# A decoder layer on one core: the finished half's stream goes through two PSUM banks, copied by ScalarE and added from there by VectorE

## What is computed

```
x = x + mamba(layernorm(x))                     # selective scan, 16 states, 512 inner channels
x = x + cross_attention(layernorm(x), ctx)      # 154 context tokens
x = ffn(x):                                     # 8 experts, top 2
    xc = x.astype(bfloat16)
    ...
    combined = sum over experts of weight_e * p2_e
    out_ffn = xc + combined.astype(bfloat16)     # a bfloat16 sum
x = x + out_ffn                                  # float32
```

## Time and profile before

| | us |
|---|---|
| median of 3 runs (1624.03 to 1624.16) | 1624.06 |
| the profiled execution, its own time | 1627.51 |
| span of the profiled execution | 1625.7 |
| DVE busy in the span | 1412.4 (87%) |
| PE / POOL / ACT busy | 1246.4 / 972.3 / 950.8 |
| mean granted PE clock | 0.902 |

### The profile page before, as it was taken

How to read it: one execution, slowest core, us unless ns; L and a number is a source line. 1 busy time by engine, 2 the same in 40 slices (tenths; PEclk the granted TensorE clock), 3 DMA queues, 4 the chain that set the end, 5 groups by cost and what they waited for, 6 DMA issues and landing times. The chain is left out here.

```text
span 1625.7 us, 24035 instructions
## 1 busy us (share of the span) xinstructions
PE 1246.4 (77%) x5942; PEld 852.6 (52%) x5942; DVE 1412.4 (87%) x1861; ACT 950.8 (58%) x1401; POOL 972.3 (60%) x529
## 2 busy tenths in 40 slices
PE   4756667779787868898777868788777777886797
PEld 2344444655455545665355545566345555565475
DVE  6589999797799999988699999989689999983697
ACT  2555444244777767524777767814777867722564
POOL 1298888312789878521689878721488978820000
PEclk9879999889798989999799989999889989997699
DMA  7111111401121211311112113221111211220111
GB/s 229 41 46 40 52 58 40 157 1 54 48 75 53 72 59 58 113 42 54 40 46 71 48 53 104 81 76 34 47 59 46 71 46 59 84 101 27 45 60 52
DMA packets 75758, 103.30 MB, mean 64 GB/s; under 512 B 9213, under 2 KB 52614, under 8 KB 75663
## 3 DMA queue, kind: packets, MB, share of 16 engines
q1 hardware_dynamic: 70508, 98.41, 19.1%
q10 hardware_dynamic: 5154, 3.78, 0.7%
HBM read 83.22 MB, written 18.96 MB: 63 GB/s over the span
## 5 line engine op out<-in xcount | busy, mean ns | idle before, releaser
L1804 PE MATMUL ps<-ident,work 128*128 128x128 f32 x1536 | 304.4, 321 | 214.4 <-DVE stage L1404 72.8
L1366 DVE TENSOR_TENSOR_SCAN work<-ps,work 128x1024 f32<-128x1024 f32 x192 | 438.4, 2283 | 27.7 <-ACT ps L966 20.2
L1804 PEld LDWEIGHTS ps<-ident,work 128*128 128x128 f32 x1536 | 191.8, 159 | 350.2 <-DVE stage L1404 124.6
L966 ACT ACTIVATE ps<-dt,a_neg 128x1024 f32<-128x1024 f32 x256 | 285.6, 1118 | 135.6 <-DVE work L1366 85.4
L719 POOL TENSOR_TENSOR work<-dtu,b_bc 128x1024 f32<-128x1024 f32 x128 | 301.8, 2385 | 50.4 <-PE ps L1804 46.5
L1404 DVE SCALAR_TENSOR_TENSOR stage<-ps,c_tok,stage 128x512 f32<-128x512 f32 x384 | 272.2, 733 | 22.2 <-PE ps L1804 20.1
L1826 PE MATMUL ps<-w,work 128*128 (+1 forms) x1024 | 249.5, 389 | 1.8 <-DVE work L1539 1.8
L1826 PEld LDWEIGHTS ps<-w,work 128*128 128x128 f32 x1024 | 195.9, 195 | 38.2 <-DVE work L1539 2.6
L735 POOL TENSOR_TENSOR stage<-stage,work 128x512 f32<-128x512 f32 x128 | 160.7, 1277 | 53.1 <-ACT work L982 53.1
L1776 PE MATMUL ps<-nfT,w 128*128 128x512 bf16 x512 | 165.8, 423 | 33.7 <-DVE work L1472 19.9
L719 POOL TENSOR_TENSOR work<-dtu,w_out 128x1024 f32<-128x1024 f32 x64 | 149.3, 2353 | 47.0 <-PE ps L1804 47.0
(11 more groups left out here) (169 smaller groups left out, 2017.0 us busy)
## 6 DMA issues: line engine op xcount, KB each, us to landing
b_bc<-b_rows SPq DMA_DIRECT2D x32, 512.0 KB, 3.9
w_out<-b_rows SPq DMA_DIRECT2D x32, 512.0 KB, 4.4
wbc<-combine_rows SPq DMA_DIRECT2D x64, 256.0 KB, 3.7
work<-z_rows SPq DMA_DIRECT2D x8, 1024.0 KB, 6.4
z_rows<-mix SPq DMA_DIRECT2D x24, 256.0 KB, 2.7
stage<-in_x SPq DMA_DIRECT2D x8, 512.0 KB, 4.3
xt<-in_x SPq DMA_DIRECT2D x8, 512.0 KB, 3.8
x_rows<-xt SPq DMA_DIRECT2D x4, 1024.0 KB, 4.3
```

The source lines that it names most:

```text
L966: act.activation(decay_in(d, alone, opening), dt[:, d, :], ACT.Exp, scale=a_neg[:, bass.ds(it * 2 + (d * N + hf * (N // 2) + par), 1)]).th ...
L1366: dve.tensor_tensor_scan(h, decays, h, 0.0, ALU.mult, ALU.add).then_inc(scan_done, 1)
L1804: mm = pe.transpose(ps[:, a % HT_BANKS, d * P:(d + 1) * P], slot(par, d)[:, a * P:(a + 1) * P], ident[:, :])
```

## The change

Four edits, cut to their core, without the declarations of the semaphores `res_banked` and `res_summed` (`bank_res` and its call are ACT's, `add_banked` DVE's, the last piece is PE's):

```diff
+                def bank_res(half):
+
+                    if half == 0:
+                        wait_apart(act, res_loaded, bp * 32 + 16)
+                    wait_apart(act, hT_used, state(b, 1, 0, 1) * SUMMED - 1 + half + HT_CREDIT)
+                    act.activation(ps[:, half, :], res[:, half * 2:half * 2 + 2, :].rearrange("p a d -> p (a d)"), ACT.Copy
+                                   ).then_inc(res_banked, 1)
...
                     decay(b, bp is None, hf, it, par, 3)
+                    second = hf == 1 and isinstance(it, int) and par == 1
                     if bp is None:
                         keep_folded(n * FOLD_STEP + 1, (n + 1) * FOLD_STEP)
                     else:
+                        if second:
+                            bank_res(0)
                         chains[1][1]()
+                        if second:
+                            bank_res(1)
...
                         dve.wait_ge(mix_taken, bp * 2 + hf + 2)
-                        dve.scalar_tensor_tensor(mix[:, :], mix[:, :], 1.0, flat16, ALU.mult, ALU.add
-                                                 ).then_inc(mix_added, 1)
+                        dve.tensor_tensor(mix[:, :], mix[:, :], flat16, ALU.add).then_inc(mix_added, 1)
...
+                def add_banked(half):
+
+                    cols = slice(half * HALF, (half + 1) * HALF)
+                    if half == 0:
+                        dve.wait_ge(mix_added, bp * 2 + 1)
+                    wait_apart(dve, res_banked, bp * 2 + half + 1)
+                    ins = dve.scalar_tensor_tensor(res[:, :, :].rearrange("p a d -> p (a d)")[:, cols], ps[:, half, :], 1.0,
+                                                   mix[:, cols], ALU.mult, ALU.add)
+                    ins.then_inc(out_ready if half else res_summed, 1)
...
                         linear_product(s, par, 0)
                         if second:
-                            for part in range(2, 5):
-                                finalize(0, part)
+                            finalize(0, 2)
                     scan(w, par, 3, decay_in(3, bp is None))
                     accumulate(hf, it, par, 7)
                     if bp is not None:
+                        if second:
+                            add_banked(0)
                         gate_product(s, 1)
+                        if second:
+                            add_banked(1)
...
-                    transposes_of((0, 1))
+                    if bp is not None and hf == 1 and not isinstance(it, int) and par == 0:
+                        pe.wait_ge(res_summed, bp + 1)
+                        transposes_of((0,))
+                        pe.wait_ge(out_ready, bp * 2 + 1)
+                        transposes_of((1,))
+                    else:
+                        transposes_of((0, 1))
```

More of the change, by code:

```diff
@@ L287, in decoder_layer @@
         mix_taken = sem("mix_taken")
+        res_banked = sem("res_banked")
+        res_summed = sem("res_summed")
         out_ready = sem("out_ready")
```

## The result

| | before | changed |
|---|---|---|
| first comparison, median (lowest to highest) | 1624.05 (1622.07 to 1624.16), 4 runs | 1611.44 (1611.40 to 1611.51), 4 runs |
| second comparison (e12) | 1626.20 (1622.11 to 1630.06), 9 runs | 1607.81 (1607.36 to 1611.46), 5 runs |
| ratio, first, with 95% interval | | 0.9921 [0.9904, 0.9938] |
| ratio, second, with 95% interval | | 0.9893 [0.9875, 0.9912] |
| span, DVE busy, mean PE clock of the profiled execution | 1625.7, 1412.4, 0.902 | 1609.6, 1396.4, 0.905 |

The kernel is faster by 12.6 us in the first comparison; 1609.6 was forecast, within 1606.5 to 1616.0. Single executions of one kernel lie up to 8 us apart, so a total says little about differences of a few microseconds. At the changed place the distance to the next scan 0 repeats to 0.02 us in all rows and profiles, of the kernel before as of the changed one, and the reading goes by it.

A forecast was written before the change was run, and what follows sets the result against it. DVE was taken to bound the loop, its adds blocked by POOL's products. Three rows at 4.13 us (12.4) plus four bfloat16 adds (2.1) made 14.5: 1627.5 to 1613.0, less 3.45 for the median, 1609.6; range 1606.5 to 1616.

The forecast's parts named there:

- Bound and cause: In the loop DVE is full; its two float32 SBUF adds stand behind POOL's products, taking 2.71 and 2.82 us.
- Bfloat16 add: Before scan 3: the plain two-input add takes 0.69 us instead of 1.22, plus a 0.18 us wait in the loop.
- The rival at 1.22: The plain bfloat16 add is no faster than the old form: 3.7 us less gain, 1613.3 us; chance 0.08.
- Banked adds: DVE's float32 adds behind tile 7's accumulation, one input in PSUM, take 0.68 us each.
- The rival that they contend too: Banked adds also meet POOL's products: 1612.2 us if the first does, 1619.7 if both take 2.8; chance 0.04.
- ACT's chain: Second copy (0.69 us) starts 0.22 behind tile 7's accumulation, then linear_in, decay 0; scan 0 comes 4.13 us earlier.
- Gain kept behind scan 0: After scan 0, the next accumulation hangs on decay 0 as before; 4.13 us a row kept, 12.4 over three rows.
- Row ends: Bfloat16 add at three row ends gives 0.53 us each; with the last row's final one, 2.1 us.
- the add that I had counted at nothing: Fifth bfloat16 add, in the last row: DVE waits behind it for ACT and PE; otherwise 0.5 us more.
- Sum: Whole kernel: 12.4 us from three rows plus 2.1 from row ends and the final add, 14.5 us; 1609.6 forecast.
- Range: Total between 1606.5 and 1616 us; the upper end is 1613.3 with row ends giving nothing, 1615.4, taken as 1616.
- the rival "no faster": The plain bfloat16 add stays at 1.22 us: 7 x 0.53 = 3.7 us less gain, 1613.3 us; chance 0.08.

The follow-up runs named there:

- e12: The changed kernel again, unaltered, in five rounds against the kernel before: 1607.81 us against 1626.20, ratio 0.9893.
- e9: Kernel before, adds still from SBUF before scan 3, with one more wait: POOL's third product waits in rows 1 to 3 until they are done; 1611.78 us.
- e1: Kernel before with the plain bfloat16 add alone; float32 adds stay in SBUF before scan 3; 1617.51 us.
- e3: Changed kernel with the two late adds reading the stream from SBUF, without ACT's copies or PE's waits for the banks; 1610.58 us.
- e7: Kernel before with one more 128x128 transpose on PE at the very start; 1624.22 us, ratio 0.9994 to the kernel before.
- e8: Changed kernel with one more 128x128 transpose on PE at the very start; 1609.01 us.
- e4: Changed kernel with ACT's second copy placed behind linear_in instead of before it; 1609.53 us.
- e6: Changed kernel with ACT's second copy made twice, the second time behind its own completion; 1608.85 us.
- e11: Changed kernel with both halves through bank 0: first added before scan 3, second copied during scan 3 and added before the gate product; 1609.59 us.
- e2: Changed kernel with the old form of the bfloat16 add, so the banks alone; 1615.95 us.

## Why the prediction was right

1. *Bound and cause* (DVE fills the loop, and stands behind POOL's products): right. e9 shows it with one wait. e1 agrees but would not show it alone: the adds keep their 2.71 and 2.82 us since POOL's products end earlier by as much as the adds start earlier. (The 96 operations that the prediction calls gate products, line 1472, are the linear products; they do have one input in PSUM, so the argument stands.) The Trainium skill's rule (SBUF — State Buffer, "Who interferes with whom") says that of a DVE operation with two SBUF inputs and a GpSimd one that reads SBUF the later blocks until the other is done. By that rule e3's late adds had to contend and e9's not, and the trace agrees: 2.29 and 1.15 us, 0.69 and 0.68.
2. *Bfloat16 add:* 0.85 us for 0.87 in the loop, 0.69 elsewhere (688 ns in the median), the lower bound taken. The rival at 1.22 fell. The Trainium skill (VectorE: DVE Perf Modes, "The perf-mode tier table") gives `tensor_tensor` twice the rate on bfloat16 in SBUF that it has on float32, and the trace agrees: 688 ns, where the float32 one of as many columns takes 1226.
3. *Banked adds:* 0.68 forecast, 0.674 to 0.678 measured in six. The rival that they contend too fell, though the first one stood beside a product (574.21 to 576.57) and the second met its last 0.57 us.
4. *ACT's chain:* right in order and place; the copy was put at 0.69 and took 0.58 to 0.60, and it started 0.12 us behind the accumulation where I took 0.22. Scan 0: 6.41 forecast, 6.17 measured.
5. *Gain kept behind scan 0:* here I was short. I had the next accumulation hang on decay 0 as before. It no longer waits: PE stood idle 3.57 us instead of 8.18, and came back to its full clock sooner, as the rows below show. Gain a row: 4.13 forecast, 4.37 at scan 0, and 4.91, 4.85 and 4.75 at scan 1. That the clock makes the difference, e12 shows in the same kernel: in its row 1 the transposes of tiles 2 and 3 take 0.63 us a pair, not 0.38, the granted clock is still 0.50 from 3 to 6 us behind the start of PE's first tile (1.00 in the first profile), and scan 1 comes 4.56 us behind scan 0 instead of 4.11; before the change it was 4.64. So this part of the gain depends on the clock. Why it came back later there, with PE idle 3.58 us as in the other, stays open. At the row's last scan 4.7 us a row are kept (4.6 in e12).
6. *Row ends:* of three counted, two gave 0.53 us (the next add starts 1.24 us behind the bfloat16 add before, 0.72 now). In the third DVE waits for PE in any case: its last add to `xt` stood for 0.27 us in the kernel before and for 0.80 now (second fence below), 0.53 more. In the last row, the add that I had counted at nothing gave nothing (40.64 us from it to the final one, before and after).
7. *Sum.* By the places it is 3 x 4.84 (the mean of the three) + 3 x 0.53 = 16.1 us; forecast 14.5. The first comparison gave 12.6, the second 18.4. The forecast of 1609.6 lies between the two medians of the changed kernel, 1611.44 and 1607.81. Its closeness is in part luck: the gain was forecast 1.6 us too small, and it was taken from 1624.06, at the low end of the medians that the kernel before showed (1624.05 to 1626.20), so the two errors are of opposite sign. The two profiled executions lie 16.1 us apart as well, but not for these terms alone: row 0 took back 2.4 us and other stretches gave as much, as said below.
8. *Range.* Its upper end was added up wrongly. The 1613.3 of the rival "no faster" already has the row ends at nothing (4 of its 7 x 0.53), so 1615.4 counts them twice; 1613.3 was the bound. The measured 1611.44 and 1607.81 lie within either.

For point 5, PE's timeline of the changed kernel in row 1, the norm's products and the transposes of tiles 2 and 3:

```profile
577.71 1.06 PE L1803 MATMUL ps<-nfT,w 128*128 128x512 bf16 x2
578.57 0.46 PE L1831 MATMUL ps<-ident,work 128*128 128x128 f32 x2
578.87 0.38 PE L1831 MATMUL ps<-ident,xt 128*128 128x128 f32 x2
579.09 0.38 PE L1831 MATMUL ps<-ident,work 128*128 128x128 f32 x2
579.30 0.38 PE L1831 MATMUL ps<-ident,xt 128*128 128x128 f32 x2
```

The first tiles behind the pause still take 0.63 to 0.69, the pace of the lower level; from 578.57 on a pair takes 0.38.

For point 6, DVE's timeline of the changed kernel at the third row end:

```profile
1444.12 0.42 DVE L1233 TENSOR_TENSOR xt<-xt,ps 128x256 f32<-128x256 f32 x1 [0.80 <-PE ps L1640]
```

What stays open is why single executions gain and lose their 2 to 8 us; where they do, the traces show. Part of it lies in row 0, which the change doesn't touch. Three stretches of the changed kernel there (columns as in the earlier trace rows, PEclk the third from the end):

```profile
60.00:130.00 70.00, 49.35 (x187) 30.61 (x187) 55.95 (x48) 42.35 (x54) 55.74 (x31) 0.83 0.08 27
130.00:200.00 70.00, 46.84 (x263) 33.71 (x262) 65.44 (x51) 33.88 (x47) 60.01 (x31) 0.90 0.17 49
200.00:280.00 80.00, 55.27 (x292) 38.40 (x290) 74.75 (x60) 38.83 (x51) 68.36 (x36) 0.87 0.17 50
```

The granted PE clock is 0.83, 0.90 and 0.87; in the kernel before the same stretches had 0.88, 0.95 and 0.94. The changed kernel reached the changed place 2.4 us later in its span (571.19 against 568.81), and the forecast had no term for it. It does not come from the change: in e12 the same kernel had 0.88, 0.95 and 0.94 there, reached the place at 569.25, and its span is the same 2.0 us shorter (1607.6 against 1609.6). A second part lies behind the third row end, in the experts of the last row. From the bfloat16 add at that row end to the next one the kernel before took 128.29 us at a clock of 0.80, its nudged twin e7 124.11 at 0.84, with the same instructions; the changed kernel took 126.9 at 0.83 in all of its three profiles (the first, e8, e12). Differences between totals in this document carry these parts, and they are larger than most of what e1 to e12 set out to show.

## What to carry to other kernels

Where an operation's duration in the trace depends on its place (0.68 here, 2.8 there), look at what the other engines are doing beside it, by the ends: here every blocked add ended 0.54 to 0.55 us behind the end of one of POOL's products, in three kernels (before, e1, e3). Three ways out exist, and the cheapest comes first: let the other engine wait where it has slack, move the operation to where the other is idle, or take one input out of SBUF. Judge such an edit by distances within the trace, and by one far enough behind the place; with single executions 8 us apart, a total can't tell 2 us. Laid beside the changed kernel's first 1611.44, four of these (e3, e4, e6, e11) would have been called gains by it, and three of them are losses at the row's last scan (0.5 to 1.0 us a row), one is level.

## What the runs showed that I had not expected

- The copy of 128x512 float32 from SBUF to PSUM on ACT takes 0.58 to 0.60 us, less than the 0.65 of ACT's operations within PSUM.
- A wait that PE is given can count for more than its length: it delays the tile, and in e2 and e6 the work behind it also ran longer at the lower clock (0.63 us for two transposes instead of 0.38). e2 lost 0.96 us a row at scan 1 for 0.54 at scan 0, e6 0.93 for 0.73. That the wait is what kept the clock low is not shown: row 1 of e12 had the same without one.
- POOL's small additions contend as well (e3: 3.39 us for two instead of 2.50), so a DVE operation with two SBUF inputs has to be kept clear of all of POOL's work, not of its long products alone.
